# One number in the expert stage: VectorE multiplies three of four half tiles, ScalarE and GpSimd one

## What is computed

```python
sim = jnp.einsum('bthpd,hkpd->pbthk', q, keys)
s1, i1 = jax.lax.top_k(sim[0], K)
s2, i2 = jax.lax.top_k(sim[1], K)
...
final_scores, pk = jax.lax.top_k(all_scores, K)
final_idx = jnp.take_along_axis(all_idx, pk, axis=-1)
wd = expert_down[final_idx]
wu = expert_up[final_idx]
hidden = jnp.einsum('btd,bthkd->bthk', x_norm, wd)
hidden = jax.nn.gelu(hidden, approximate=False)
hidden = hidden * jax.nn.relu(final_scores)
out = jnp.einsum('bthk,bthkd->btd', hidden, wu)
```

## Time and profile before

| | us |
|---|---|
| median of three runs | 2496.89 (2482.84 to 2497.84) |
| the profiled execution | 2491.81 |
| its span | 2490.1 |
| busy in the span: PE / DVE / ACT / POOL | 1924.0 / 1714.5 / 670.6 / 461.2 |
| mean granted clock of TensorE | 0.875 |
| POOL L1540, 96 instructions, busy | 154.1 |
| DVE L1875, 100 instructions, busy | 68.1 |

### The profile page before, as it was taken

One profiled execution on the slowest core, in us unless ns is written; L12 is line 12 of the kernel. 1 busy time (PEld: TensorE's weight loads), 2 busy tenths in 40 slices (PEclk: granted clock), 3 DMA queues, 4 the chain that ended last, 5 costly groups with the idle time before them and its releaser, 6 DMA issues. The chain is left out here.

```text
span 2490.1 us, 48756 instructions
## 1 busy us (share of the span) xinstructions
PE 1924.0 (77%) x17712; PEld 1559.4 (63%) x17712; DVE 1714.5 (69%) x7029; ACT 670.6 (27%) x1478; POOL 461.2 (19%) x670
## 2 busy tenths in 40 slices
PE   6585899974678878779778797797786997559991
PEld 3364788853567767668667676686675675236661
DVE  3343666635999999989989989999974775510003
ACT  2342455543212112122121121221211554102210
POOL 2003344320020120220202202102122100130004
PEclk8696999987789989889898898898887999669995
DMA  2103444305300000000000000000002331413313
GB/s 58 30 26 84 106 108 102 92 2 138 73 1 6 1 6 6 2 6 5 2 6 1 6 6 1 6 2 2 1 1 55 86 82 26 146 52 121 113 53 110
DMA packets 86758, 107.70 MB, mean 43 GB/s; under 512 B 26462, under 2 KB 75230, under 8 KB 85790
## 3 DMA queue, kind: packets, MB, share of 16 engines
q1 hardware_dynamic: 81056, 96.62, 14.7%
q0 software_dynamic: 3296, 6.43, 0.9%
q10 hardware_dynamic: 2176, 1.61, 0.2%
HBM read 70.61 MB, written 30.51 MB: 41 GB/s over the span
## 5 line engine op out<-in xcount | busy, mean ns | idle before, releaser
L1611 PE MATMUL peer_out_ps<-peer_g,peer_up 128*128 128x256 f32 (+1 forms) x1664 | 377.9, 392 | 84.7 <-issue 76.8
L1611 PEld LDWEIGHTS peer_out_ps<-peer_g,peer_up 128*128 128x128 f32 x1664 | 325.8, 203 | 133.2 <-issue 84.8
L1576 PE MATMUL peer_x_ps<-peer_xc,peer_dt 128*128 128x256 f32 (+1 forms) x1664 | 355.0, 374 | 26.7 <-DMA peer_up<-in_L_ffn_expert_up_dram 19.1
L1576 PEld LDWEIGHTS peer_x_ps<-peer_xc,peer_dt 128*128 128x128 f32 x1664 | 308.1, 192 | 68.5 <-issue 28.5
L1540 POOL TENSOR_TENSOR peer_g<-peer_g,peer_qt 128x512 f32<-128x512 f32 x96 | 154.1, 1643 | 802.4 <-ACT peer_qt L1702 802.4
L1680 ACT ACTIVATE peer_g<-peer_x_ps 128x512 f32<-128x512 f32 (+1 forms) x208 | 119.1, 572 | 645.3 <-PE peer_x_ps L1576 645.2
L1277 DVE TENSOR_REDUCE l_attn_mx<-l_attn_s_ps 98x4 f32<-98x392 f32 (+1 forms) x320 | 175.0, 560 | 140.9 <-PE l_attn_s_ps L1047 101.0
L1600 PE MATMUL peer_x_ps<-peer_oh_h,peer_oh_a 128*128 128x32 bf16 x3136 | 171.3, 181 | 112.6 <-DVE peer_oh_l L1868 96.6
L1600 PEld LDWEIGHTS peer_x_ps<-peer_oh_h,peer_oh_a 128*128 128x128 bf16 x3136 | 164.9, 99 | 129.8 <-DVE peer_oh_l L1868 64.9
L1861 DVE TENSOR_TENSOR peer_oh_a<-peer_a_t,peer_iota_f 128x8192 bf16<-128x8192 bf16 x49 | 216.6, 4420 | 1.3
L1198 ACT ACTIVATE l_attn_pt<-l_attn_st_ps 98x392 f32<-98x392 f32 x320 | 148.0, 491 | 149.1 <-PE l_attn_st_ps L1060 148.2
(11 more groups left out here) (310 smaller groups left out, 3464.9 us busy)
## 6 DMA issues: line engine op xcount, KB each, us to landing
moe_w<-in_L_ffn_w_dram SPq DMA_DIRECT2D x16, 1024.0 KB, 9.1
l_attn_pieces_q_dram<-l_attn_pieces_q SPq DMA_DIRECT2D x16, 294.0 KB, 4.4
l_attn_pieces_k_dram<-l_attn_pieces_k SPq DMA_DIRECT2D x16, 294.0 KB, 3.1
l_attn_stq<-l_attn_pieces_q_dram SPq DMA_DIRECT2D x16, 294.0 KB
l_attn_stk<-l_attn_pieces_k_dram SPq DMA_DIRECT2D x16, 294.0 KB
peer_g<-n_L_ffn_expert_down_dram SPq DMA_DIRECT2D x8, 512.0 KB, 6.8
peer_up<-in_L_ffn_expert_up_dram SPq DMA_DIRECT2D x2, 2048.0 KB
l_xi<-net_x SPq DMA_DIRECT2D x16, 196.0 KB, 2.4
```

The source lines that it names most:

```text
L1576: mm = nc.tensor.matmul(x_ps[b][:, jj * CT:jj * CT + cols], dt[:, k, 2 * jp + jj, :], xc[p][:, k, 0:cols], start=(k == 0), stop=(k == KC - 1))
L1611: mm = nc.tensor.matmul(out_ps[:, m * CT:m * CT + cols], up[:, j, m * P:(m + 1) * P], g[:, j, 0:cols], start=(j == 0), stop=(j == J - 1))
```

## The change

`LATE` goes from 2 to 3. Everything else that reads it follows: which half tiles `weigh` does on VectorE, how many quarters ScalarE copies and GpSimd multiplies, and the numbers that the waits count to.

```diff
-    LATE = NHB // 2
+    LATE = NHB - 1
```

## The result

The change makes the kernel slower: 2527.4 us (2524.89 to 2531.05, four runs) against 2495.55, a ratio of 1.0139 with an interval of 1.0102 to 1.0177. Measured again beside 22 runs of the kernel before it is 2521.36 (2509.19 to 2525.59, seven runs), ratio 1.0082 (1.0055 to 1.0109). The forecast was 2505, the range ended at 2519; two of the seven runs, at 2509, lie inside it.

The account below looks back on a forecast made before the run. A ring through the wait at L1839 bounds the kernel, TensorE slightly late and VectorE close behind. 2491.81 + 0.5 (ring and last step) + 13.6 (clock) = 2505.9, stated as 2505; range 2489 to 2519.

Parts of the forecast that it names:

- The ring: VectorE and TensorE waiting on each other through L1839, chunks 0 to 11: multiplications cost 25.0, 22.7 fills waits, net +2.3 us.
- The last step: Step from chunk 11 to the rest: GpSimd stands idle beside VectorE's one-hots instead of slowing them, -1.8 us.
- The clock at the turn: TensorE's longer pause at the turn lowers its clock, late hidden values delay VectorE: 1.7 us in eight chunks, 13.6.
- the upper bound: Clock loss per chunk at the turn: 4.5 us at half speed, 2.25 us more.
- That the clock holds: Rival at the turn: TensorE's clock stays up despite the doubled pause, only the ring counts, 2492; chance 0.20.
- that the multiplications are hidden: Rival on VectorE: the added multiplications cost nothing, GpSimd's shorter path gains 19 us, 2473; chance 0.05.
- The slower rival: TensorE's clock stays at 1.2 GHz through the whole late part, 10.4 us in each of eight chunks, 2573; chance 0.09.

Follow-up runs that it names:

- the kernel with LATE = 2 and both edits: Changed kernel at LATE = 2, second token tile's turn behind two late hidden pairs, last outputs over 128 columns: 2495.01 us, ratio 0.9998.
- the run with the second turn later: Changed kernel with the second token tile's turn moved behind two pairs of late hidden values, on TensorE and ScalarE: 2504.94 us, ratio 1.0019.

## Why the prediction was wrong

- **The ring.** Right. The multiplications filled the wait at L1839 down to 1.73 to 1.97 us (1.93 forecast). GpSimd's four took 5.9 us, the outputs of chunk 3 began 7.8 us behind the scatter (7.7), the turn waits 3.15 in chunk 3 (3.3). A chunk without a fall of the clock takes 99.75 us, where 98.9 + 1.0 = 99.9 was forecast. One reading was too small: the queue's pause at the three jumps was 2.34, 2.46 and 2.82 us, and I took the shortest for all.
- **The last step.** GpSimd and VectorE no longer collide: the last L1868 of chunk 11 takes 1.22 us instead of 2.50. The step was forecast at -1.8 plus 1.7 of clock and measured at +0.4, mainly since that chunk waited 2.56 at L1875, 0.86 more than the 1.7.
- **The clock at the turn.** The mechanism was right, the size at the upper bound. I took 1.7 us for eight chunks; L1875 waited 1.8 to 2.6, 2.24 on average, in nine, all but chunks 6 and 8. With the ring that makes 17.05 us for the eleven steps, where 2.3 + 7 x 1.7 = 14.2 were expected, the eighth being chunk 11. What I had not read is where the clock fell before the change. In its three profiles the 2.65 us brought it down at 6 of 33 turns, and all six stand in chunks 4, 6 and 8, where the pause at the loop's jump lies ahead of them.
- **The step that failed** is the sum's end: the rest of 64 tokens does not stand in it at all. I followed the ring to its last L1839 and took what comes behind it as unchanged, though I had argued that the clock depends on when TensorE works. It costs 10.8 us in each of three profiles. Without it the profiled execution would have taken 2514.6, inside the range; but the forecast with it is 2516.7, still inside, so it needs the other terms to get out: 2505.9, 10.8 for the rest, 17.05 - 14.2 = 2.9 for the ring (the waits at L1875 rose by 15.3 where 7 x 1.7 = 11.9 were set), and 0.5 for the last step come to 2520, one above the range's end. The remaining 5 us of the profile's 2525.41 lie outside the stage.
- **What stays open.** Some 5 us of the 33.6 lie outside the stage (4.2 ahead, 1.1 behind), in instructions that the change leaves alone. In three profiles each the first L1839 starts at 668.1, 672.8 and 666.2 before, and at 672.3, 673.9 and 672.0 after, and with edits that touch nothing ahead of it anywhere from 662.6 to 675.0. No run parts a cause from chance here.
- **The rivals.** That the clock holds is refuted by the profile; that the multiplications are hidden by the run without them. The slower rival came at another place than I had put it: not in the late hidden values, where the clock was back after some 5 us, but in the last outputs, where it did not come back. It had 0.09.

## What to carry over

When two engines take turns as the later one, work moved between them fills waits at first, and the engine that now comes early stands idle: ask what idleness does to its clock, and look for work that can stand in the pause, as two pairs of hidden values did here: they gave back 2.7 us a chunk, more than the fallen clock took, halved its stay at 1.2 GHz, and seldom kept it up. Follow a change to the last instruction of the stage, odd-sized remainder included, and look at the clock there too. At 2.4 GHz 128 products of 64 columns took 14.51 us and 128 of 128 columns 14.56, so widening the narrow ones cost nothing here.

## What was not expected of the hardware

- The granted clock fell when TensorE had been busy without a gap for 2.5 us: at 1893 in the changed kernel, in products of 64 columns, and it stayed at 1.2 GHz for the 23 us until they ended. The pause ahead of the first product, 0.78 us, can have a part in the fall; behind the same pause the clock held with 128 columns. With 128 columns the same number of products took 14.56 us at 2.4 GHz. The Trainium skill, "TensorE: Matmul & The Clock Gate", section "HAM oscillation — how this bites in real kernels", tells of waits between groups that bring the clock down; the turns agree with that, at nine of eleven after the change. For a low clock through 23 us without a wait only these runs speak.
- A small shift went with 10.8 us: a clock that rose 0.4 to 0.54 us before the last outputs of 64 columns held (four profiles), one that rose 0.64 to 0.9 us before them fell again within 4 us (four profiles).
- At a jump of the loop TensorE's queue stood still for 2.2 to 3.1 us in these profiles. That pause alone can bring the clock down, as at 1254 in the kernel with LATE = 2 and both edits.
- Whether the clock holds is not told by the length of the one pause: 2.65 us brought it down at 6 of 33 turns of the kernel before, all behind a jump, and in the run with the second turn later it held behind 3.1 and 3.2 us and fell behind 2.2.
